# One tap moved from VectorE, two-bank gelus, scales in the weights and a new order of steps in a Mamba and feed-forward layer

## The chip, the cores and the metric

One Trainium2 chip, one core. The time is that of the whole program on the device, in microseconds. The engines are TensorE (PE in the profile, its weight loads PEld), VectorE (DVE), ScalarE (ACT), GpSimd (POOL) and SyncE (SP), which here only issues DMAs.

## The reference

One layer on x of 32 sequences x 256 steps x 128 channels, all in float32:

```
xz = x @ W_in.T ;  u, z = split(xz)                       # 256 inner channels each
u  = silu(causal_conv(u, 4 taps per channel) + conv_b)
B, C, d = split(u @ W_x.T)                                # 16, 16 and 1 columns
dt = softplus(d * W_dt + b_dt)
h[t] = exp(dt[t] * A) * h[t-1] + (u[t] * dt[t]) * B[t]    # 256 channels x 16 states
y  = sum_over_states(h * C) + u * D ;  y = (y * silu(z)) @ W_out.T
x1 = layernorm(x + y)
a  = silu((x1 @ w1) * s1) * ((x1 @ w2) * s2)              # 512 hidden
a  = gelu((a @ h1) * t1) ;  a = gelu((a @ h2) * t2)
out = layernorm(x1 + (a @ w3) * s3)
```

The w, h matrices are ternary numbers times 8; s1, s2, t1, t2 are scales of one number for each hidden column.

## The kernel before, in words

The 8192 rows are cut into NB = 16 blocks of TB = 512 columns (two sequences), with channels on the 128 partitions. The state of one block is 256 x 16 = 4096 rows, that is 32 tiles of 128 partitions, handled in 16 steps `v` of two tiles each.

Every engine runs the same `rounds`: round j runs over the 16 steps, scans block j, and lays the other stages of four other blocks between its steps: the intake of block I = j+2 (first projection and convolution), the front of block A = j+1 (z, the rows of B and C, dt), the back of F = j-1 (out projection, norm, gate and up projections, the first hidden layer h1, the start of h2), and the tail of T = j-2 (rest of h2, w3, last norm, store). The order on each engine is written out by hand as `if v == ...` lines in each engine's `run`. Engines meet only in semaphores.

In one step, VectorE makes two products U = X * xdr (L765; X is the PSUM bank that holds B for the step's states, xdr comes by DMA) and two scans hb = scan(dA, U) (L778). ScalarE makes dA = exp(dtr * negA) (`decay`, L456) some eight tiles ahead (AHEAD), in a ring of DA_RING = 10. GpSimd multiplies both hb by C (`output_term`, L384) into pb, and TensorE sums them over states into bank Y0 or Y1 (`sum_group`, L853). X is refilled three times a round by ScalarE (`fill_X`, L466): fill 0 needs the last U of the round before, and VectorE's first U of the next round needs fill 0.

The convolution of inner channels 0 to 127 is done on VectorE: ScalarE writes the first tap with the bias into `conv` (`conv_first`, L470) and VectorE adds three more, reading the projection in its bank (`taps`, L714). For channels 128 to 255 ScalarE makes the products of all taps (`conv_second`, L480 and L486) into `xtap`, slices 1 to 3 of `hid`, and GpSimd adds them (`add_tap`, L398).

The norm of the first half goes over four engines: `out_proj` (TensorE, L906), `variances` (ScalarE, L559), `rsqrt` (GpSimd, L389 and L391), `scaled` into `x1` (VectorE, L728), `turn_x1` (TensorE, L913), a copy into `x1T` (ScalarE, L656). Then TensorE makes the gate and up projections (L866, L869), ScalarE the silu and a scaled copy (L677, L680), GpSimd their product (L423), TensorE the hidden layers (`hidden`, L862: four outputs m of four matmuls each), and ScalarE a gelu of each bank (L554), whose `scale` is a column of `sc_sb`. `add_x1` (L886) and `down` (L894) end the tail's matmuls. The last norm's residual is read from x1T too, two rounds after it was written for block T, before block F's copy overwrites it.

Silu, gelu and exp lie in different function tables of ScalarE; the profile shows an ACT_TABLE_LOAD at each switch.

The DMAs of a round are all issued by SP in one order: among them store_steps (dts and xds to DRAM), spread_steps (dtr and xdr, 256 KB each, back in replicated form), spread_B and spread_C.

Of the kernel before, what the change touches and what calls it, by code (L numbers as in the profile page):

```python
# [37 lines left out]

CW, CB, DP, WD, BD = 0, 4, 5, 6, 7
# [6 lines left out]

def states_of(k):

    return (0, 0, 1, 1, 1, 1, 0, 0)[k]


def build(nc, xT, win, wx, chp, alog, cwrow, sel, rep, wout, w1, w2, h1, h2, w3, scales, cent_in, ident_in, out):
    with ExitStack() as ctx:
# [19 lines left out]
        sc_sb = sb("sc_sb", [P, 5, NH])  # L73
        negA = sb("negA", [P, TILES])
        sel_sb = sb("sel_sb", [P, PARITIES, 2 * SD])
        rep_sb = sb("rep_sb", [P, PARITIES, P])
        diagD = sb("diagD", [P, NC, P])
# [32 lines left out]

        xtap = hid[:, 1:TAPS, :]
        yo = sb("yo", [P, NT, DM])
# [11 lines left out]
        Y = [ps(f"Y{c}", [P, TB]) for c in range(NC)]  # L124
        G = [ps(f"G{i}", [P, TB]) for i in range(3)]
# [4 lines left out]
        s_zero, s_aexp, s_aneg = sem("s_zero"), sem("s_aexp"), sem("s_aneg")  # L130
        s_sc, s_raw, s_w3x, s_wop, s_wo, s_w3p, s_w3c = (sem("s_sc"), sem("s_raw"), sem("s_w3x"), sem("s_wop"), sem("s_wo"),
# [4 lines left out]
        s_ip, s_conv0, s_tap, s_c1, s_xs = sem("s_ip"), sem("s_conv0"), sem("s_tap"), sem("s_c1"), sem("s_xs")  # L136
        s_conv1, s_xtap, s_tap1 = sem("s_conv1"), sem("s_xtap"), sem("s_tap1")
# [25 lines left out]
        def x_of(b):  # L163

            return x1T[:] if b == 1 else xT_sb[:]
# [8 lines left out]
        G0, G1, G2, Y0, Y1 = G[0][:], G[1][:], G[2][:], Y[0][:], Y[1][:]  # L174
# [9 lines left out]
        BH2 = (G1, G2, G0, G1)  # L184

# [43 lines left out]
        def _(sp):  # L229
# [30 lines left out]
            sp.dma_start(rep_sb[:], rep).then_inc(s_rep, 16)  # L260
# [4 lines left out]
            sp.dma_start(sc_sb[:], scales).then_inc(s_sc, 16)  # L265
            load_xT(1)
            sp.wait_ge(s_rows, 1)
# [28 lines left out]
            sp.dma_start(w1_sb[:], w1).then_inc(s_weights, 16)  # L296
            sp.dma_start(w2_sb[:], w2).then_inc(s_weights, 16)
            sp.dma_start(h1_sb[:], h1.rearrange("(c p) m -> p c m", p=P)).then_inc(s_weights, 16)
# [65 lines left out]
        def _(pool):  # L364
# [80 lines left out]
        def _(act):  # L445
# [145 lines left out]
            for u in range(2):  # L591
                decay(0, u)
# [536 lines left out]
```

## Time and profile before

| | |
|---|---|
| times of three runs | 1041.04, 1045.28, 1045.74 us (median 1045.28) |
| profiled execution | 1041.06 us, of it the span of the instructions 1039.2 us |
| granted TensorE clock | 0.974 of full speed, mean over the span |
| moved by DMA | 184.13 MB, mean 177 GB/s |

Busy time is the time in which an engine has at least one instruction at work; on TensorE the ends of matmuls are modelled. A round can be measured as the distance between two equal instructions of neighbouring rounds. An instruction's duration is some 0.1 us longer than the distance to the next one, since neighbours overlap; costs are therefore best taken from distances.

### The profile page before, as it was taken

The page shows a single profiled execution, that of the slowest core. Times are in us where ns is not written, and L with a number is a line of the kernel's source. Part 1 is how long each engine was busy: PE and PEld are TensorE (multiplying, and loading weights), DVE is VectorE, ACT ScalarE, POOL GpSimd, SP SyncE. Part 2 cuts the span into 40 slices and gives each one's busy share as a digit, 9 for nine tenths or more (in the row PEclk, how much of TensorE's full clock was granted, in tenths as well). Part 3 has the DMA queues.
Part 4 walks back from the last instruction along what each step waited for, and adds up shares of the span by engine and source line. Part 5 has one row for each costly group of instructions (what it writes and reads, how often), then busy time and mean ns, then how long its engine had stood idle before and what let it go on. Part 6 is the DMA issues. An engine that isn't in the chain of part 4 may idle for free.

```text
span 1039.2 us, 13592 instructions
## 1 busy us (share of the span) xinstructions
PE 967.8 (93%) x3852; PEld 428.7 (41%) x3852; DVE 952.1 (92%) x1143; ACT 909.6 (88%) x1544; POOL 841.5 (81%) x497
## 2 busy tenths in 40 slices
PE   5956899999999999999999999999999999998998
PEld 2313335353444435343443535344443534444454
DVE  2899999999999999999999999999999999999500
ACT  5397799999999999999999999999999999997342
POOL 1478898979889897989889897988989798988420
PEclk8688899999999999999999999999999999999999
DMA  4959294784829386593939478392948657392000
GB/s 138 277 175 295 73 294 122 206 233 125 268 88 303 96 244 192 157 267 91 284 84 306 126 200 239 114 274 84 292 114 239 199 155 251 90 301 71 0 11 10
DMA packets 110428, 184.13 MB, mean 177 GB/s; under 512 B 12944, under 2 KB 23696, under 8 KB 110352
## 3 DMA queue, kind: packets, MB, share of 16 engines
q1 hardware_dynamic: 109824, 182.94, 61.1%
q8 instruction: 30, 0.49, 0.2%
q14 instruction: 46, 0.38, 0.1%
q10 hardware_dynamic: 528, 0.32, 0.1%
HBM read 161.19 MB, written 22.02 MB: 176 GB/s over the span
## 4 chain that ended last, share of the span: by engine, by line
PE 26%; issue 24%; DVE 22%; ACT 22%; POOL 5%; DMA 0%; ACTq 0%; DVEq 0%; POOLq 0%; SPq 0%
DVE hb L778 11%; ACT dA L456 9%; DVE U L765 8%; PE G L862 6%; PE G L894 4%; PE Y L853 3%; PE G L866 2%; POOL pb L384 2%; PE Y L862 2%; ACT hid L486 2%; PE G L869 2%; POOL hid L423 1%; ACT xds L519 1%; PE Y L869 1%; ACT dts L519 1%
## 5 line engine op out<-in xcount | busy, mean ns | idle before, releaser
L384 POOL TENSOR_TENSOR pb<-hb,crep 128x1024 f32<-128x1024 f32 x256 | 602.2, 2363 | 110.1 <-DVE hb L778 99.5
L778 DVE TENSOR_TENSOR_SCAN hb<-dA,U 128x512 f32<-128x512 f32 x512 | 595.0, 1205 | 0.0
L456 ACT ACTIVATE dA<-dtr,negA 128x510 f32<-128x510 f32 x500 | 320.9, 711 | 5.9 <-DVE hb L778 5.4
L765 DVE TENSOR_TENSOR U<-X,xdr 128x512 f32<-128x512 f32 x500 | 319.4, 686 | 3.6 <-ACT X L466 2.4
L862 PE MATMUL G<-g,h_sb 128*128 128x512 f32 x512 | 234.2, 601 | 0.0
L862 PE MATMUL G<-hid,h_sb 128*128 128x512 f32 x384 | 173.1, 601 | 0.8 <-ACT g L680 0.8
L853 PE MATMUL Y<-pb,sel_sb 128*32 128x512 f32 x1024 | 138.9, 614 | 19.0 <-POOL pb L384 19.0
L862 PEld LDWEIGHTS G<-g,h_sb 128*128 128x128 f32 x512 | 93.6, 190 | 138.1 <-issue 136.4
L862 PEld LDWEIGHTS G<-hid,h_sb 128*128 128x128 f32 x384 | 70.5, 190 | 103.7 <-issue 101.9
L423 POOL TENSOR_TENSOR hid<-hid,g 128x512 f32<-128x512 f32 x64 | 80.7, 1272 | 13.8 <-ACT g L680 13.7
L853 PEld LDWEIGHTS Y<-pb,sel_sb 128*32 128x32 f32 x1024 | 20.7, 108 | 98.3 <-issue 64.6
L554 ACT ACTIVATE hid<-G,sc_sb 128x512 f32<-128x512 f32 x64 | 40.9, 684 | 20.9 <-PE G L862 20.6
L862 PE MATMUL Y<-hid,h_sb 128*128 128x512 f32 x128 | 57.5, 592 | 0.0
L554 ACT ACT_TABLE_LOAD x44 | 56.5, 1283 | 0.8
L894 PE MATMUL G<-w_sb,hid 128*128 128x128 f32 x480 | 56.1, 275 | 0.0
L456 ACT ACT_TABLE_LOAD x43 | 55.2, 1283 | 0.8
L894 PEld LDWEIGHTS G<-w_sb,hid 128*128 128x128 f32 x480 | 54.8, 192 | 0.2 <-issue 0.2
L866 PE MATMUL G<-x1T,w_sb 128*128 128x512 f32 x96 | 51.5, 619 | 0.0
L398 POOL TENSOR_TENSOR conv<-conv,hid 128x510 f32<-128x510 f32 (+2 forms) x42 | 48.2, 1148 | 2.7 <-ACT hid L486 2.6
L367 POOL TENSOR_TENSOR dts<-dts,xds 128x512 f32<-128x512 f32 x30 | 38.3, 1276 | 5.2 <-ACT xds L526 5.2
L677 ACT ACTIVATE hid<-G,sc_sb 128x512 f32<-128x512 f32 x48 | 32.9, 685 | 9.2 <-PE G L866 8.1
L374 POOL TENSOR_TENSOR xds<-dts,xs 128x512 f32<-128x512 f32 x31 | 39.4, 1272 | 1.3
(141 smaller groups left out, 1116.5 us busy)
## 6 DMA issues: line engine op xcount, KB each, us to landing
dtr<-scr_dt SPq DMA_DIRECT2D x252, 256.0 KB, 7.2
xdr<-scr_xd SPq DMA_DIRECT2D x252, 256.0 KB, 7.1
brep<-scr_rows SPq DMA_DIRECT2D x32, 256.0 KB, 6.1
crep<-scr_rows SPq DMA_DIRECT2D x32, 256.0 KB, 8.1
scr_dt<-dts SPq DMA_DIRECT2D x32, 256.0 KB, 4.3
scr_xd<-xds SPq DMA_DIRECT2D x32, 256.0 KB, 4.2
xres<-xT_d SPq DMA_DIRECT2D x16, 256.0 KB, 5.5
xT_sb<-xT_d SPq DMA_DIRECT2D x15, 256.0 KB, 2.7
```

Of the source, the lines that this page charges most:

```text
L374: nc.gpsimd.tensor_tensor(xds[:, c, :], dts[:, c, :], xs[:, b % 2, c, :], ALU.mult).then_inc(s_xd, 1)
L384: nc.gpsimd.tensor_tensor(pb[:, qs:qs + 2, :], hb[:, hs:hs + 2, :], crep[:, b % 2, g:g + 1, :].to_broadcast([P, 2, TB]), ALU.mult).then_in ...
L398: nc.gpsimd.tensor_tensor(acc, acc, halves(xtap[:, s - 1, :])[:, :, 0:SEQ - s], ALU.add).then_inc(s_tap1, 1)
L423: nc.gpsimd.tensor_tensor(hid[:, m, :], hid[:, m, :], up[:, m, :], ALU.mult).then_inc(s_hid, 1)
L456: nc.scalar.activation(halves(dA[:, decay_slot(b, u), :])[:, :, 1:SEQ], halves(BREP[q] if by_product(b, k) else dtr[:, slot, q, :])[:, :, ...
L554: nc.scalar.activation(o[:, m, :], banks[m], ACT.Gelu, scale=sc_sb[:, kind, m:m + 1]).then_inc(s_done, 1)
L765: nc.vector.tensor_tensor(U[i][:], X[:], xdr[:, slot, q + i, :], ALU.mult).then_inc(s_u, 1)
L778: nc.vector.tensor_tensor_scan(hb[:, 2 * (v % H_PAIRS) + i, :], dA[:, decay_slot(j, u), :], U[i][:], 0.0, ALU.mult, ALU.add).then_inc(s_h, 1)
L853: last = nc.tensor.matmul(Y[c][rows32, :], sel_sb[:, e, :], pb[:, (GT * k + q) % (2 * P_PAIRS), :], start=False, stop=(k % (GROUPS // NC) ...
L862: last = nc.tensor.matmul(to, w[:, k, m * P:(m + 1) * P], x[:, k, :], start=(k == 0), stop=(k == NH - 1))
L866: nc.tensor.matmul(BGATE[m], w1_sb[:, m * P:(m + 1) * P], x1T[:], start=True, stop=True).then_inc(s_ga, 1)
L894: last = nc.tensor.matmul(tile_of(BW3, t), tile_of(g2[:, k, :], t), w3_sb[:, k, :], start=False, stop=(k == NH - 1), skip_group_check=True)
```

## The change

It does these things at once.

- **Scales.** s1, s2, t1, t2 are multiplied into w1, w2, h1, h2 once by GpSimd (`scale_plain`, `scale_hidden`), from rows `srow` broadcast by DMA into g1. Silu, copy and gelu then have no scale operand. w1, w2, h1 and the rows are loaded at the start; h2 later.
- **Gelu.** One instruction for two adjacent banks (G and Y are now one tensor GY), 128x1024, in all rounds that scan. Those of h1 are placed after decay tile 32 instead of at step 11.
- **Tap.** From block 2 on, one of VectorE's three taps is taken away: ScalarE writes its product into slice 0 of hid (`tap_first`), GpSimd adds it to conv (`add_tap0`), before VectorE's other two.
- **x1T** has two buffers.
- **Orders.** `rsqrt` of the first norm at step 3 instead of 4; `scaled` into x1 before the U pair of step 5 instead of behind it; turn_x1 before add_x1; out_proj before z_proj; fill_X(A, 0) after decay tile 34 instead of ahead of tile 36; fill_X(j, 2) between Abs and Relu; conv_first at step 13; hidden output 2 of h1 at step 10, ahead of a sum_group; at the start, negA and the first four decays before the second half's softplus.
- **Small.** The two silus of the convolution are one, 128x1024. rep_sb and diagD share memory with other tensors.

```diff
+POOL_TAPS = 1
+def taps_before(b):
+    return 3 * b if b < 2 else 6 + (3 - POOL_TAPS) * (b - 2)
-        x1T = sb("x1T", [P, TB])
+        x1T = sb("x1T", [P, 2, TB])
+        srow = g1
+        xtap0 = [hid[:, 0, :]]
+        GY = ps("GY", [P, 3 + NC, TB])
+        G, Y = [GY[:, i, :] for i in range(3)], [GY[:, 3 + c, :] for c in range(NC)]
+        BH1_2 = (GY[:, 0:2, :], GY[:, 2:4, :])
+        BH2_2 = (GY[:, 1:3, :], GY[:, 0:2, :])
...
             load_xT(1)
+            sp.dma_start(flat(srow[:, 0:3, :]), scales[:, 0:3 * HID].to_broadcast([P, 3 * HID])).then_inc(s_weights, 16)
+            sp.dma_start(w1_sb[:], w1).then_inc(s_weights, 16)
+            sp.dma_start(w2_sb[:], w2).then_inc(s_weights, 16)
+            sp.dma_start(h1_sb[:], h1.rearrange("(c p) m -> p c m", p=P)).then_inc(s_weights, 16)
...
+            def add_tap0(b, i):
+                pool.wait_ge(s_conv0, b + 1)
+                pool.wait_ge(s_xtap0, POOL_TAPS * (b - 2) + i + 1)
...
+                nc.gpsimd.tensor_tensor(acc, acc, halves(xtap0[i])[:, :, 0:SEQ - s], ALU.add).then_inc(s_tap0, 1)
+            def scale_plain(w, i):
+                pool.wait_ge(s_weights, 16 * 4)
+                nc.gpsimd.tensor_tensor(w[:], w[:], srow[:, i, :], ALU.mult).then_inc(s_wsc, 1)
+            def scale_hidden(w, i, half):
...
+                o = w[:, 2 * half:2 * half + 2, :]
+                nc.gpsimd.tensor_tensor(o, o, srow[:, i:i + 1, :].to_broadcast([P, 2, HID]), ALU.mult).then_inc(s_wsc, 1)
...
-                    if v == 4 and back:
+                    if v == 3 and back:
                         rsqrt(var1, ve1, rs1, s_var1, F + 1, s_rs1, 2 * F + 2)
...
+                    if v == 15 and intake and back:
+                        for i in range(POOL_TAPS):
+                            add_tap0(I, i)
+                    if v == 0 and j == 1:
+                        for i in range(POOL_TAPS):
+                            add_tap0(A, i)
...
+                    if v == 13 and j == 0:
+                        scale_hidden(h2_sb, 3, 0)
+                    if v == 15 and j == 0:
+                        scale_hidden(h2_sb, 3, 1)
                     if scan:
                         output_term(j, v)
...
+            def tap_first(b):
+                if b > 2:
+                    act.wait_ge(s_h1, 4 * (b - 3) + 4)
+                for i in range(POOL_TAPS):
+                    nc.scalar.activation(xtap0[i], bank_in(b), ACT.Copy, scale=chp_sb[:, 0, CW + i:CW + i + 1]).then_inc(s_xtap0, 1)
...
+            def gelu(o, bank2, s_in, s_done, b, m, n):
+                if o is g2 and b + 3 < NB:
+                    act.wait_ge(s_tap1, 3 * (b + 1) + m + n - 1)
+                act.wait_ge(s_in, 4 * b + m + n)
+                nc.scalar.activation(flat(o[:, m:m + n, :]), bank2, ACT.Gelu).then_inc(s_done, n)
...
-                    if v == 14 and front:
-                        fill_X(A, 0)
+                    if v == (13 if back else 14) and intake:
+                        conv_first(I)
+                        tap_first(I)
...
+                        if u == 32 and back and scan:
+                            gelu(g1, flat(BH1_2[0]), s_h1, s_g1, F, 0, 2)
+                            gelu(g1, flat(BH1_2[1]), s_h1, s_g1, F, 2, 2)
+                        if u == 34 and front:
+                            fill_X(A, 0)
...
-                            silu_conv(A, 0)
-                            silu_conv(A, 1)
+                            nc.scalar.activation(flat(xs[:, A % 2, :, :]), flat(conv[:]), ACT.Silu).then_inc(s_xs, 2)
...
-                        softplus_lines(A, 1)
-                        fill_X(j, 2)
+                        softplus_lines(A, 1, lambda: fill_X(j, 2))
...
             def taps(b):
-                for s in range(1, TAPS):
+                moved = POOL_TAPS if b > 1 else 0
+                for s in range(1, TAPS - moved):
...
+                    if moved:
+                        dve.wait_ge(s_tap0, POOL_TAPS * (b - 1))
...
+                        if v == 5 and back:
+                            scaled(x1, BOUT, rs1, s_rs1, 2 * F + 2).then_inc(s_x1, 1)
                         k, q = divmod(2 * v, GT)
...
-                    if v == 0 and front and j > 0:
+                    if v == (0 if tail else 1) and front and j > 0:
                         taps(A)
...
+                    if v == 2 and back:
+                        out_proj(F)
                     if v == (2 if back else 4) and front:
...
+                    if v == 4 and back:
+                        turn_x1(F)
                     if v == 4 and tail:
...
+                    if v == 10 and back:
...
+                        hidden(BH1[2], h1_sb, 2, hid, s_hid, s_h1, F)
```

## Rows read from the trace of the kernel before

**Rows 1.** Stages: length, busy PE, PEld, DVE, ACT, POOL, then clock, DMA.

```profile
486.00:545.50 59.50, 57.78 (x238) 25.63 (x237) 59.33 (x72) 57.25 (x98) 53.09 (x32) 1.00 0.71 192
```

**Rows 2.** Timeline of VectorE: start, us, what, idle time before it.

```profile
89.96 2.28 DVE L714 SCALAR_TENSOR_TENSOR conv<-Y,chp_sb,conv 128x510 f32<-128x510 f32 x3
...
148.66 2.29 DVE L714 SCALAR_TENSOR_TENSOR conv<-Y,chp_sb,conv 128x510 f32<-128x510 f32 x3
...
505.58 2.28 DVE L714 SCALAR_TENSOR_TENSOR conv<-Y,chp_sb,conv 128x510 f32<-128x510 f32 x3
507.78 1.29 DVE L765 TENSOR_TENSOR U<-X,xdr 128x512 f32<-128x512 f32 x2
508.97 2.32 DVE L778 TENSOR_TENSOR_SCAN hb<-dA,U 128x512 f32<-128x512 f32 x2
...
522.06 1.27 DVE L765 TENSOR_TENSOR U<-X,xdr 128x512 f32<-128x512 f32 x2
523.24 0.68 DVE L728 TENSOR_TENSOR x<-Y,rs 128x512 f32<-128x512 f32 x1
...
559.20 2.33 DVE L778 TENSOR_TENSOR_SCAN hb<-dA,U 128x512 f32<-128x512 f32 x2
561.61 1.30 DVE L765 TENSOR_TENSOR U<-X,xdr 128x512 f32<-128x512 f32 x2
```

**Rows 3.** Timeline of TensorE, the same round.

```profile
522.39 0.66 PE L886 MATMUL G<-ident,x1T 128*128 128x128 f32 x4 [0.40 <-ACT hid L554]
523.98 0.66 PE L913 MATMUL Y<-ident,x 128*128 128x128 f32 x4 [0.93 <-DVE x L728]
...
548.38 1.06 PE L853 MATMUL Y<-pb,sel_sb 128*32 128x512 f32 x8 [0.29 <-POOL pb L384]
```

**Rows 4.** Groups of ScalarE's instructions: count, busy us, mean ns.

```profile
L554 ACT ACTIVATE hid<-G,sc_sb 128x512 f32<-128x512 f32 x64 | 40.9, 684 | 20.9 <-PE G L862 20.6
...
L500 ACT ACTIVATE zs<-G 128x512 f32<-128x512 f32 x32 | 18.8, 588 | 0.9 <-PE G L819 0.9
...
L496 ACT ACTIVATE xs<-conv 128x512 f32<-128x512 f32 x31 | 17.9, 622 | 0.2
...
L505 ACT ACTIVATE zs<-zs 128x1024 f32<-128x1024 f32 x16 | 16.7, 1047 | 0.0
```

**Rows 5.** Timeline of ScalarE around the gelus of h1 and fill 0.

```profile
556.54 0.69 ACT L554 ACTIVATE g<-Y,sc_sb 128x512 f32<-128x512 f32 x1 [0.80 <-PE Y L862]
557.25 1.28 ACT L456 ACT_TABLE_LOAD   x1
558.54 2.55 ACT L456 ACTIVATE dA<-dtr,negA 128x510 f32<-128x510 f32 x4
561.00 0.58 ACT L466 ACTIVATE X<-brep 128x512 f32<-128x512 f32 x1
```

**Rows 6.** Timeline of GpSimd, end of round 0 and a middle round, and a group.

```profile
80.62 9.31 POOL L384 TENSOR_TENSOR pb<-hb,crep 128x1024 f32<-128x1024 f32 x4
...
508.90 1.11 POOL L398 TENSOR_TENSOR conv<-conv,hid 128x508 f32<-128x508 f32 x1
...
L398 POOL TENSOR_TENSOR conv<-conv,hid 128x506 f32<-128x506 f32 x14 | 15.2, 1083 | 0.0
```

**Rows 7.** Issues of dtr (500 to 565 us), the first one's and all landing times.

```profile
546.62 2.45 SPq L257 DMA_DIRECT2D dtr<-scr_dt  x4
...
dtr<-scr_dt SPq DMA_DIRECT2D x1, 256.0 KB, 3.1
...
DMA to landing us min/median/max: 3.1/7.8/10.6
```

**Rows 8.** The start, in TensorE's and ScalarE's timelines.

```profile
18.79 1.23 PE L918 MATMUL G<-dts,rep_sb 32*128 32x512 f32 x3 [3.76 <-DVE dts L738]
...
20.99 1.26 ACT L456 ACTIVATE dA<-G,negA 128x510 f32<-128x510 f32 x2
```

**Rows 9.** VectorE's timeline behind its last scan.

```profile
982.75 0.69 DVE L723 TENSOR_TENSOR gT<-Y,zs 128x512 f32<-128x512 f32 x1 [7.01 <-PE Y L853]
```

More of the change, by code:

```diff
@@ L518, in softplus_lines @@
                 for f, o in ((ACT.Abs, soft), (ACT.Relu, dts)):
+                    if between is not None and f == ACT.Relu:
+                        between()
                     nc.scalar.activation(o[:, c, :], BDT, f, bias=chp_sb[:, c, BD:BD + 1],
@@ L589, in _ @@
             act.wait_ge(s_aneg, 1)
+            act.wait_ge(s_dtb, 1)
+            softplus_part(0, ACT.Abs)
+            softplus_part(0, ACT.Relu)
+            softplus_rest(0)
             act.wait_ge(s_zero, 3)
-            for u in range(2):
+            softplus_part(1, ACT.Abs)
+            softplus_part(1, ACT.Relu)
+            for u in range(GT):
                 decay(0, u)
+            softplus_rest(1)
             fill_X(0, 0)
-            for u in range(2, AHEAD):
+            for u in range(GT, AHEAD):
                 decay(0, u)
@@ L616, in run @@
                             decay(A, u - TILES)
+                        if u == 32 and back and scan:
[3 more added lines that the diff above has]
+                            fill_X(A, 0)
+                    if v == 11 and back and not scan:
+                        for m in range(NH):
+                            gelu(g1, BH1[m], s_h1, s_g1, F, m, 1)
                     if v == 3 and scan:
@@ L640, in run @@
                     if v == 1 and tail:
-                        gelu(g2, 3, BH2, s_h2, s_g2, T, (0, 1))
-                    if v == 1 and scan and j > 0:
+                        if scan:
+                            gelu(g2, flat(BH2_2[0]), s_h2, s_g2, T, 0, 2)
+                        else:
+                            for m in (0, 1):
+                                gelu(g2, BH2[m], s_h2, s_g2, T, m, 1)
+                    if v == (1 if tail else 2) and scan and j > 0:
                         start_sum(j, 0)
@@ L646, in run @@
                     if v == 4 and tail:
-                        gelu(g2, 3, BH2, s_h2, s_g2, T, (2, 3))
+                        if scan:
+                            gelu(g2, flat(BH2_2[1]), s_h2, s_g2, T, 2, 2)
+                        else:
+                            for m in (2, 3):
+                                gelu(g2, BH2[m], s_h2, s_g2, T, m, 1)
                     if v == 5 and front and not back:
@@ L691, in run @@
                     if v == 8 and front:
-                        softplus_lines(A, 1)
-                        fill_X(j, 2)
+                        softplus_lines(A, 1, lambda: fill_X(j, 2))
                         softplus_logs(A, 1)
-                    if v == 14 and intake:
-                        conv_first(I)
-                    if v == 11 and back:
-                        gelu(g1, 2, BH1, s_h1, s_g1, F, range(NH))
                     if v == 15 and intake and not back:
@@ L765, in run @@
                                 nc.vector.tensor_tensor(U[i][:], X[:], xdr[:, slot, q + i, :], ALU.mult).then_inc(s_u, 1)
-                        if v == 5 and back:
-                            scaled(x1, BOUT, rs1, s_rs1, 2 * F + 2).then_inc(s_x1, 1)
                         if v == 9 and tail:
@@ L992, in run @@
                             add_x1(T)
-                    if v == 4 and back:
-                        turn_x1(F)
                     if v == 4 and tail and j <= NB:
@@ L1064, in run @@
                         in_proj(I)
-                    if v == 11 and back:
-                        if front:
-                            pe.wait_ge(s_pre, 4 * A)
-                        hidden(BH1[2], h1_sb, 2, hid, s_hid, s_h1, F)
                     if v == 12 and back:
```

108 lines of the change are left out of this document (51 added, 57 removed).

## The prediction

> **What bounds the kernel now.** I read the busy time by stage first [rows 1]. A middle round of 59.5 us has VectorE busy for 59.33 us, TensorE for 57.78, ScalarE for 57.25 and GpSimd for 53.09: VectorE has no room, TensorE and ScalarE have some 2 us each, GpSimd 6.
>
> Next I read VectorE's timeline [rows 2]. From the taps at 148.66 to those at 505.58 lie six rounds, 356.92 us, so a round is 59.49. The first such distance, from 89.96 to 148.66, is 58.70: that round has no last norm. Three taps cost 2.20 us (505.58 to 507.78), 0.735 each. There is one short wait: the pair of scans begun at 559.20 would let the next U begin 2.24 us later (its 2.33 less some 0.09 of overlap), at 561.44, but it begins at 561.61. It waits 0.17 us for fill 0 of X, which ScalarE ended at 561.58 [rows 5]. So two loops are closed at almost the same length: VectorE's own work, 59.49 - 0.17 = 59.32 us, and a loop over TensorE and ScalarE that ends in that fill.
>
> The second loop is seen in TensorE's and ScalarE's timelines [rows 3, 5]. TensorE waits 0.40 us for a gelu of h2 before add_x1, 0.93 for x1 from VectorE, and 0.29 for pb at 548.38; otherwise it works on until the last output of h1, whose gelu begins at 556.54. Then come a table load, four decays and fill 0, and VectorE's U, taps and x1 close the loop. Whoever shortens VectorE's work alone meets this loop at once.
>
> **The change, part by part.**
>
> *Tap.* VectorE loses 0.735 us in rounds 1 to 14, where blocks 2 to 15 are convolved: 14 x 0.735 = 10.3 us. ScalarE gains one copy from a bank with a scale: 684 ns like its gelus [rows 4], less 0.08 of overlap, 0.61. GpSimd gains one add, 1.08 us [rows 6]; its 53.1 becomes 54.2 of 58.6. The add stands at step 15 ahead of an output_term. What hides it is GpSimd's idle time, 6 us a round, and that TensorE's sum of this term is two hidden outputs away; with GpSimd full, all behind it would come 1.08 us later.
>
> *x1 and TensorE's order.* `scaled` moves ahead of a pair of U, so x1 is 523.24 - 522.06 = 1.18 us earlier [rows 2], if rs1 is there; rsqrt at step 3 sees to that. Out_proj ahead of z_proj feeds ScalarE's variances, which ScalarE reaches later anyway: zero. turn_x1 ahead of add_x1 puts add_x1's 0.5 us behind x1. Output 2 of h1 ahead of the sum hides the wait of 0.29 [rows 3]. From fill 0 over x1 to the last output of h1 that is -0.735 - 1.18 + 0.5 - 0.29 = -1.7 us.
>
> *Gelus and fill 0.* A two-bank gelu isn't in the trace. From below it is one bank without scale, 588 ns, and what 512 more columns cost, 1047 - 622 = 425 ns: 1.01 us; from above it is two of today's, 1.37 [rows 4]. I take 1.05, the row of the same width. In place of 0.69 it adds 0.36 us behind the last output of h1. Then table load, one decay, conv_first (0.66, a copy like the tap's), tap_first and one more decay are 1.28 + 0.62 + 0.66 + 0.61 + 0.62 = 3.79 us up to fill 0, against 561.00 - 557.25 = 3.75 now [rows 5]. Fill 0 is 0.4 us later behind the last output of h1, and the loop over fill 0 and x1 is 59.49 - 1.7 + 0.4 = 58.2 us.
>
> A third loop runs over the gelus of h2. ScalarE's way from the last output of h1 to the gelu for which add_x1 waits changes by 0.36, + 0.61 for tap_first, - 0.62 for decay 32, which now lies ahead, + 0.04, - 0.2 for the first pair of h2, + 0.45 since add_x1 waits for a whole pair: + 0.65. TensorE's way behind it loses the turn and the wait for x1: add_x1 to the end of turn_x1 is 523.98 + 0.5 - 522.39 = 2.1 us now and 0.5 then, -1.6, and the 0.29 [rows 3]. That loop is 59.49 + 0.65 - 1.9 = 58.25 us.
>
> *VectorE's own loop* is then 59.32 - 0.735 = 58.58 us, 0.3 above both. The margin is thin, but VectorE stays the bound, and its 0.17 us wait for fill 0 goes too, in 13 rounds (2 to 14): 2.2 us.
>
> The Trainium skill (Perfetto Trace Analysis, Optimizing Scalar/DVE Operations) says the reverse of the merge: where ScalarE isn't saturated but causes bubbles on other engines, breaking instructions up may let work be done sooner. The 0.40 us before add_x1 is such a bubble. By that rule the third loop, which the merge lengthens, would decide; this is the first rival.
>
> *Scales.* Four silus and four copies a round lose 0.1 us each (684 against 588 ns, rows 4), but ScalarE waits there for TensorE's next bank: zero in the rounds. In the last chain some three of them lie on the way: -0.3 us.
>
> *Fill 2* comes one softplus line earlier; VectorE wasn't seen waiting for it: zero.
>
> *Decay 32 ahead of the gelus.* It needs the first dtr of the next block, issued at 546.62 and landed 3.1 us later, at 549.7 [rows 7]. ScalarE gets there at 552.6 (556.54, less its wait of 0.80, three gelus of 0.6 and the table load). Covered by 2.9 us: zero.
>
> *Start.* The first decays began at 20.99, with all of the softplus ahead of them; the replicated dts is there at 18.79 + 1.2 = 20.0 [rows 8]. They start then: -1.0 us. The loads of 2.4 MB that move ahead of the first rows of B and C take 13 us at the page's mean of 177 GB/s, and about half in a burst; I take them as hidden behind the convolution and softplus of block 0, and keep 3 us, once, for the range. Scaling w1, w2, h1 costs GpSimd 2 x 1.27 + 2 x 2.33 = 7.2 us while it has nothing else.
>
> *h2 at the end of round 0.* Here GpSimd isn't idle: four output_terms from 80.62 to 89.93 [rows 6], 2.33 each, the last of them 3.5 us behind its scans. Two scalings (2.33 each) and add_tap0 (1.08) are put ahead of its next work: add_tap0 ends at 89.93 + 4.66 + 1.08 = 95.7, less 1.0 from the start, 94.7. VectorE's taps of block 2, now one step later, would start at 89.96 + 3.42 - 1.0 = 92.4 [rows 2]. They wait 2.3 us: +2.3, once. The bounds are 0, if GpSimd's lag is taken up earlier, and 3.5.
>
> *End.* When the scans end TensorE is further ahead by 1.18 + 0.29 - 0.5 = 0.97 us, and the chain behind the last scan is TensorE's: the gate waits 7.01 us for it [rows 9]. I take -0.9, and the -0.3 above.
>
> Sum: -10.3 - 2.2 - 1.0 + 2.3 - 1.2 = -12.4 us. The profiled execution took 1041.06 us (span 1039.2 and 1.9 around it), which gives 1028.7. The median of the three runs is 1045.28, 4.2 above the profiled one, and would give 1032.9; the three runs lie at both ends of that gap (1041.04, 1045.28, 1045.74). I take the middle, 1043.2, less 12.4: 1031.
>
> **The rivals.**
>
> *ScalarE and TensorE decide the round.* If the two-bank gelu takes 1.37 us, the loop over fill 0 gets 0.3 longer and the loop over the gelus of h2 1.0, as three pairs stand in it: 59.2 against 58.58. For it speaks how thin the margins are; against it that the same width in SBUF took 1047 ns. It costs 13 x 0.6 = 8 us of the gain: 1039.
>
> *GpSimd's add blocks VectorE.* Each add_tap0 would hold VectorE for its 1.08 us, 14 x 1.08 = +15.1, and the sum is +2.7: 1046. Against it: a pair of scans beside such an add (508.97, the add from 508.90) took 2.32 us, like one elsewhere (559.20, 2.33) [rows 2, 6]. The Trainium skill (the same section) warns that the two share an SBUF read port, so that offloading between them might not help; by it this rival would hold.
>
> *Slower: dtr comes too late for decay 32.* The place is ScalarE ahead of the gelus of h1; their delay reaches TensorE's next matmuls and fill 0. 2.9 us are covered by today's landing, 0.8 by ScalarE's present wait for the last output of h1, 0.3 by the margin of the loops. From a landing of 3.1 + 4.0 = 7.1 us on, each further us costs one in each of 13 rounds; at 8.1 us the gain is gone. The landings of dtr in that stretch have median 7.8 and maximum 10.6 us [rows 7]. With 10.6 it is 13 x 3.5 = 45 us worse: 1076. Against it: the first piece starts the burst and meets an empty queue, since it follows GpSimd's dt.
>
> *No effect.* VectorE's taps would wait for add_tap0 in every round, if GpSimd, which goes into step 15 some 1 us behind the scans, came 2 us later than now. Then start and end alone remain: 1043.2 - 1 = 1042. Against it: its 3 us of idle time around steps 0 to 3.
>
> **Numbers.** My case 0.68 (1025 to 1036 by itself), the loops 0.17 (to 1041), blocked VectorE 0.04, dtr late 0.04, no effect 0.07. The range 1023 to 1041 leaves out the last three and a little below. A measurement here can't tell less than 0.5%, 5.2 us, from no change, so faster begins below 1040. Faster 0.84, within 0.5% 0.10, slower 0.06.
>
> **What would show it.** Right: taps of two at a distance of 58.6 us in rounds 2 to 14, no wait of the first U for fill 0, one wait of some 2.3 us for add_tap0 at the first taps of two, scans that start 1 us earlier, gelus of 1.05 us. Wrong: VectorE waiting for X every round (first rival), scans over 2.4 us a pair beside L398's like (second), the exp of tile 32 waiting for a DMA (third), taps waiting for GpSimd every round (fourth). Most likely to spoil the number: a gelu over two banks above 1.1 us, or which level, 1041 or 1045, the median falls on.

## The result, and the profile after

The changed kernel takes 1033.67 us (median of five runs, 1032.09 to 1035.66) against 1045.28 (five runs, 1041.04 to 1045.74): ratio 0.9903, 95% interval 0.9879 to 0.9928. This ratio, like those below, is built from all the runs; it is that of the two means, 1033.91 and 1043.98, and not that of the two medians (0.9889). Predicted: 1031.0, range 1023 to 1041. The profiled execution took 1034.61 us, span 1032.7. One later execution of the kernel before, beside places_back and h2_in_round1, took 2471.68 us and is left out of their ratios.

**The round.** One stage of the profile of after, with the columns of [rows 1]:

```profile
481.50:540.00 58.50, 57.08 (x237) 25.43 (x236) 58.37 (x71) 55.99 (x94) 53.95 (x33) 1.00 0.75 195
```

Now VectorE's timeline of after, to be read against [rows 2]:

```profile
97.85 1.63 DVE L786 SCALAR_TENSOR_TENSOR conv<-GY,chp_sb,conv 128x510 f32<-128x510 f32 x2 [2.86 <-POOL conv L419]
...
152.47 1.60 DVE L786 SCALAR_TENSOR_TENSOR conv<-GY,chp_sb,conv 128x510 f32<-128x510 f32 x2
...
557.01 2.31 DVE L850 TENSOR_TENSOR_SCAN hb<-dA,U 128x512 f32<-128x512 f32 x2
559.25 1.26 DVE L839 TENSOR_TENSOR U<-X,xdr 128x512 f32<-128x512 f32 x2
...
855.66 1.60 DVE L786 SCALAR_TENSOR_TENSOR conv<-GY,chp_sb,conv 128x510 f32<-128x510 f32 x2
...
966.38 2.32 DVE L850 TENSOR_TENSOR_SCAN hb<-dA,U 128x512 f32<-128x512 f32 x2
976.95 0.69 DVE L795 TENSOR_TENSOR gT<-GY,zs 128x512 f32<-128x512 f32 x1 [8.24 <-PE GY L925]
```

From 152.47 to 855.66 lie twelve rounds, 58.60 us each (59.49 before). VectorE is busy for all but 0.1 us of one. The U at 559.25 follows its scans after 2.24 us, so the wait for fill 0 is gone. The taps take 1.51 us up to the next U where three took 2.20 [rows 2]: the moved tap gives back 0.69 us, not 0.735. Before the taps of round 1 there is one wait of 2.86 us for GpSimd's add.

TensorE, ScalarE and GpSimd of after, a middle round, against [rows 3, 5, 6]:

```profile
579.18 0.66 PE L985 MATMUL GY<-ident,x 128*128 128x128 f32 x4 [1.42 <-DVE x L800]
579.67 0.60 PE L958 MATMUL GY<-ident,x1T 128*128 128x128 f32 x4
```

```profile
551.67 1.02 ACT L615 ACTIVATE g<-GY 128x1024 f32<-128x1024 f32 x1
553.24 1.02 ACT L615 ACTIVATE g<-GY 128x1024 f32<-128x1024 f32 x1 [0.54 <-PE GY L934]
...
558.05 0.59 ACT L518 ACTIVATE X<-brep 128x512 f32<-128x512 f32 x1
```

```profile
559.60 1.12 POOL L419 TENSOR_TENSOR conv<-conv,hid 128x506 f32<-128x506 f32 x1
```

A gelu over two banks takes 1.02 us. Fill 0 ends at 558.64, 0.6 before its U starts. TensorE now waits for VectorE's x1 by 1.42 us and no longer for a gelu before add_x1: the slack has moved to the engines that don't set the round.

**Where the time went,** between the two profiled executions: start +2.8 us; the rest of round 0 and round 1 +1.0; twelve rounds -10.67; rounds 14 and 15 up to the end of the last scan -0.2; behind it +0.5. The sum is -6.5, which is their difference. The profiled execution of before lies at the low end of its runs and that of after near the high end of its own, so the gain between the means is larger, 10.1 us.

**The start,** VectorE and GpSimd of after:

```profile
19.35 2.19 DVE L810 TENSOR_TENSOR dts<-dts,xds 128x512 f32<-128x512 f32 x1 [8.90 <-ACT xds L598]
21.58 2.72 DVE L813 TENSOR_TENSOR xds<-dts,xs 128x512 f32<-128x512 f32 x1
26.75 1.30 DVE L835 TENSOR_TENSOR U<-GY,brep 128x512 f32<-128x512 f32 x2 [2.45 <-PE GY L990]
...
46.30 2.45 DVE L786 SCALAR_TENSOR_TENSOR conv<-GY,chp_sb,conv 128x510 f32<-128x510 f32 x3 [2.00 <-ACT conv L522]
```

```profile
16.21 2.49 POOL L423 TENSOR_TENSOR w_sb<-w_sb,g 128x512 f32<-128x512 f32 x2 [9.18 <-DMA h_sb<-h_d]
18.65 5.10 POOL L429 TENSOR_TENSOR h_sb<-h_sb,g 128x1024 f32<-128x1024 f32 x2
```

The taps of block 1 come at 46.30; before they came at 43.53. Two VectorE instructions, both of whose inputs are in SBUF, took 2.19 and 2.72 us, where they took 0.69 each before, beside GpSimd's scalings of h1, which took 2.55 each where 2.33 had been reckoned.

**The end,** TensorE of after in round 15, and the windows there (columns as in [rows 1]; the clock is the last number but two):

```profile
929.25 1.11 PE L985 MATMUL GY<-ident,x 128*128 128x128 f32 x4 [3.22 <-DVE x L800]
...
931.01 5.72 PE L966 MATMUL GY<-w_sb,hid 128*128 128x128 f32 x32
```

```profile
918.00:925.00 7.00, 7.00 (x40) 4.16 (x39) 7.00 (x9) 6.33 (x16) 4.84 (x3) 1.00 1.08 287
...
930.00:935.00 5.00, 5.00 (x25) 5.00 (x24) 5.00 (x7) 4.28 (x6) 3.39 (x2) 0.50 1.06 247
```

```profile
944.67 0.69 DVE L800 TENSOR_TENSOR yo<-GY,rs 128x512 f32<-128x512 f32 x1 [0.61 <-POOL rs L410]
```

TensorE waited 3.22 us for x1, the granted clock fell from 1.00 to 0.50 (1.2 GHz) towards the end of that wait, the down projection took 5.72 us, and VectorE (last row) then waited 0.61 us for the last norm that depends on it.

### The profile page after: what moved, and what is told of

Read it like the earlier page. It is cut to its first block, busy times and chain, and to the rows that moved or that the text cites. A ratio compares the mean times of both kernels' runs of the same rounds, so it can differ in the third digit from the quotient of the medians.

```text
span 1032.7 us, 13619 instructions
## 1 busy us (share of the span) xinstructions
PE 961.2 (93%) x3852; PEld 428.7 (42%) x3852; DVE 943.9 (91%) x1129; ACT 891.4 (86%) x1486; POOL 867.8 (84%) x517
## 4 chain that ended last, share of the span: by engine, by line
PE 51%; issue 17%; ACT 14%; DVE 11%; POOL 3%; DMA 1%; SPq 1%; ACTq 0%; DVEq 0%; POOLq 0%
PE GY L934 23%; ACT dA L508 6%; PE GY L925 6%; DVE hb L850 5%; PE GY L966 5%; PE GY L938 5%; PE GY L941 4%; DVE U L839 4%; PE GY L906 2%; ACT hid L545 2%; POOL pb L403 2%; ACT L508 1%; DVE gT L795 1%; PE GY L881 1%; PE GY L985 1%
## 5 line engine op out<-in xcount | busy, mean ns | idle before, releaser
L934 PE MATMUL GY<-g,h_sb 128*128 128x512 f32 x512 | 234.2, 601 | 0.0
L934 PE MATMUL GY<-hid,h_sb 128*128 128x512 f32 x512 | 228.7, 600 | 0.9 <-ACT g L756 0.7
L925 PE MATMUL GY<-pb,sel_sb 128*32 128x512 f32 x1024 | 138.5, 613 | 14.7 <-POOL pb L403 14.6
L934 PEld LDWEIGHTS GY<-g,h_sb 128*128 128x128 f32 x512 | 93.5, 190 | 138.2 <-issue 138.2
L934 PEld LDWEIGHTS GY<-hid,h_sb 128*128 128x128 f32 x512 | 93.6, 190 | 136.4 <-issue 122.5
L938 PE MATMUL GY<-x1T,w_sb 128*128 128x512 f32 x128 | 69.4, 624 | 0.0
L941 PE MATMUL GY<-x1T,w_sb 128*128 128x512 f32 x128 | 66.1, 599 | 0.9 <-ACT hid L754 0.9
L966 PE MATMUL GY<-w_sb,hid 128*128 128x128 f32 x480 | 58.1, 281 | 0.0
L966 PEld LDWEIGHTS GY<-w_sb,hid 128*128 128x128 f32 x480 | 56.9, 198 | 0.0
L754 ACT ACTIVATE hid<-GY 128x512 f32<-128x512 f32 x64 | 37.9, 592 | 17.2 <-PE GY L938 17.2
L615 ACT ACTIVATE hid<-GY 128x1024 f32<-128x1024 f32 (+1 forms) x36 | 33.5, 930 | 21.0 <-PE GY L934 20.7
## 6 DMA issues: line engine op xcount, KB each, us to landing
xres<-xT_d SPq DMA_DIRECT2D x16, 256.0 KB, 10.1
```

What stands on the lines that cost most here:

```text
L615: nc.scalar.activation(flat(o[:, m:m + n, :]), bank2, ACT.Gelu).then_inc(s_done, n)
L925: last = nc.tensor.matmul(GY[rows32, 3 + c, :], sel_sb[:, e, :], pb[:, (GT * k + q) % (2 * P_PAIRS), :], start=False, stop=(k % (GROUPS // ...
L934: last = nc.tensor.matmul(to, w[:, k, m * P:(m + 1) * P], x[:, k, :], start=(k == 0), stop=(k == NH - 1))
L938: nc.tensor.matmul(BGATE[m], w1_sb[:, m * P:(m + 1) * P], x1T[:, b % 2, :], start=True, stop=True).then_inc(s_ga, 1)
L941: nc.tensor.matmul(BUP[m], w2_sb[:, m * P:(m + 1) * P], x1T[:, b % 2, :], start=True, stop=True).then_inc(s_up, 1)
L966: last = nc.tensor.matmul(tile_of(BW3, t), tile_of(g2[:, k, :], t), w3_sb[:, k, :], start=False, stop=(k == NH - 1), skip_group_check=True)
```

## The experiments

Eleven kernels were run, each timed in several rounds beside the kernel before on the same chip (`after_again` is the changed kernel once more; median of before 1042.64 us for the first four, 1041.79 for the next four, then 1041.92 for two and 1041.48 for the last). The round is read as the distance of equal taps.

| kernel | median us | ratio, 95% interval | round us |
|---|---|---|---|
| tap_alone | 1039.37 | 0.9955 (0.9937 to 0.9972) | 59.18 |
| tap_back | 1042.18 | 0.9995 (0.9978 to 1.0011) | 59.42 |
| norm_order_back | 1037.35 | 0.9941 (0.9920 to 0.9963) | 58.79 |
| gelu_one_bank | 1033.77 | 0.9903 (0.9871 to 0.9935) | 58.60 |
| after_again | 1033.21 | 0.9910 (0.9894 to 0.9926) | 58.60 |
| scale_at_step4 | 1030.32 | 0.9886 (0.9869 to 0.9902) | 58.60 |
| scale_gaps_negA | 1029.98 | 0.9884 (0.9869 to 0.9899) | 58.60 |
| filler | 1030.54 | 0.9888 (0.9873 to 0.9903) | 58.60 |
| places_back | 1037.48 | 0.9950 (0.9935 to 0.9966) | 58.99 |
| h2_in_round1 | 1031.31 | 0.9891 (0.9876 to 0.9907) | 58.60 |
| wout_first | 1028.19 | 0.9864 (0.9840 to 0.9887) | 58.60 |

**1. tap_alone:** the kernel before with nothing but the tap moved.

```diff
+                    if v == 15 and intake and back:
+                        add_tap0(I, 0)
+                    if v == 0 and j == 1:
+                        add_tap0(A, 0)
...
                     if v == 14 and intake:
                         conv_first(I)
+                        tap_first(I)
...
-                for s in range(1, TAPS):
+                moved = POOL_TAPS if b > 1 else 0
+                for s in range(1, TAPS - moved):
...
-                    if s == 1:
-                        dve.wait_ge(s_conv0, b + 1)
-                    else:
-                        dve.wait_ge(s_tap, 3 * b + s - 1)
+                    dve.wait_ge(s_conv0, b + 1)
+                    if moved:
+                        dve.wait_ge(s_tap0, POOL_TAPS * (b - 1))
+                    if s > 1:
+                        dve.wait_ge(s_tap, taps_before(b) + s - 1)
```

> The kernel before with the tap moved and nothing else. Theory of the loops: a round of VectorE's own work would be 58.6 us, but the loop over ScalarE and TensorE through the gelus of h2 gets tap_first's 0.6 us on ScalarE and loses only TensorE's wait for x1, so a round becomes about 59.0 us (from 59.49) and VectorE waits some 0.4 us a round for fill 0. Total some 6 us below before. Rival (only VectorE's work counts): a round of 58.6 us, as in the full change, 11 to 12 us below before.

Measured: a round of 59.18 us, 1039.37. A tap was taken from VectorE and the round lost only 0.31 us. VectorE's timeline of tap_alone shows what holds it; the wait for GpSimd stands in each of the rounds 3 to 14:

```profile
326.43 1.63 DVE L744 SCALAR_TENSOR_TENSOR conv<-Y,chp_sb,conv 128x510 f32<-128x510 f32 x2 [0.26 <-POOL conv L406]
...
556.97 2.33 DVE L808 TENSOR_TENSOR_SCAN hb<-dA,U 128x512 f32<-128x512 f32 x2
559.39 1.30 DVE L795 TENSOR_TENSOR U<-X,xdr 128x512 f32<-128x512 f32 x2
```

The loop over the other engines did take over, and it holds VectorE in two places. Behind the scans of 556.97 the next U begins after 2.42 us, where 2.24 is enough in rounds without a wait: the short wait for fill 0 is still there, as in before. The new wait, for the add of the moved tap, is 0.34 us by the same reading. The two taps take 1.55 us for 2.20, so the round is 0.65 shorter by the tap and 0.34 longer by the new wait: the 0.31 measured. The theory had the round (59.0) nearly right, but saw only the wait at fill 0. GpSimd's timeline of tap_alone says where the new wait comes from: there the add waits for ScalarE's copy,

```profile
443.65 1.08 POOL L406 TENSOR_TENSOR conv<-conv,hid 128x506 f32<-128x506 f32 x1 [1.90 <-ACT hid L496]
```

whereas after's L419 begins right behind GpSimd's own work.

**2. tap_back:** the change without the tap.

```diff
-POOL_TAPS = 1
+POOL_TAPS = 0
```

> The changed kernel with the tap back on VectorE (three taps, no tap_first, no add_tap0). Theory: VectorE's own loop of 59.3 us sets the round, without its wait for fill 0; the 2.9 us wait for add_tap0 in round 1 is gone. So 14 x 0.735 less 2.9 = 7.4 us above the changed kernel, some 3 us below before. Rival (the orders give the time and the tap little): a round of 58.6 to 58.8 us, within 2 us of the changed kernel.

Measured: 59.42 us a round, 1042.18, no difference from before. VectorE of tap_back:

```profile
506.42 2.44 DVE L786 SCALAR_TENSOR_TENSOR conv<-GY,chp_sb,conv 128x510 f32<-128x510 f32 x3
508.77 1.29 DVE L839 TENSOR_TENSOR U<-X,xdr 128x512 f32<-128x512 f32 x2
```

The orders remove the wait for fill 0 (0.20 us a round with the slightly later U behind it). But three taps now take 2.35 us up to the next U, 0.15 more than in before. The edit left on the taps is that all but the first wait for two semaphores where one was; that this costs the 0.15 is likely, but wasn't tried apart. So this kernel isn't quite the orders alone. Neither half of the change is worth much by itself (0.31 and 0.07 us a round); together they are worth 0.89: 0.69 for the tap and 0.20 for fill 0.

**3. norm_order_back:** rsqrt at step 4, `scaled` behind the U pair, turn_x1 behind add_x1.

```diff
-                    if v == 3 and back:
+                    if v == 4 and back:
                         rsqrt(var1, ve1, rs1, s_var1, F + 1, s_rs1, 2 * F + 2)
...
-                        if v == 5 and back:
-                            scaled(x1, BOUT, rs1, s_rs1, 2 * F + 2).then_inc(s_x1, 1)
...
+                        if v == 5 and back:
+                            scaled(x1, BOUT, rs1, s_rs1, 2 * F + 2).then_inc(s_x1, 1)
...
-                    if v == 4 and back:
-                        turn_x1(F)
                     if v == 4 and tail:
...
+                    if v == 4 and back:
+                        turn_x1(F)
```

> The changed kernel with the first norm's order as before: rsqrt at step 4, scaled behind the U pair of step 5, turn_x1 behind add_x1. Theory: x1 comes 1.2 us later and add_x1's 0.5 us goes ahead of it, so the loop over x1, TensorE and fill 0 gets 0.7 us longer than its 58.2: 58.9 us a round, with VectorE waiting 0.3 us for fill 0 each round: 4 us above the changed kernel. Rival (TensorE has 1.4 us to spare at x1 and takes it up): the round stays at 58.6 us, within 1 us.

Measured: 58.79 us, 1037.35. TensorE of norm_order_back again waits ahead of add_x1, now longer than in [rows 3]:

```profile
522.91 0.66 PE L958 MATMUL GY<-ident,x1T 128*128 128x128 f32 x4 [1.62 <-ACT hid L615]
```

The order of the norm is worth 0.19 us a round. It reaches VectorE through fill 0, as the theory says. Its timeline, and ScalarE's:

```profile
558.60 2.33 DVE L850 TENSOR_TENSOR_SCAN hb<-dA,U 128x512 f32<-128x512 f32 x2
561.00 1.30 DVE L837 TENSOR_TENSOR U<-X,xdr 128x512 f32<-128x512 f32 x2
```

```profile
560.38 0.59 ACT L518 ACTIVATE X<-brep 128x512 f32<-128x512 f32 x1
```

The U begins 2.40 us after its scans instead of 2.24, right behind the fill, which ends at 560.97, and it takes 0.03 longer up to the next scans. The theory holds in kind; its 0.3 us was 0.19.

**4. gelu_one_bank:** 128x512 gelus in the same places, those of h2 too.

```diff
-                            gelu(g1, flat(BH1_2[0]), s_h1, s_g1, F, 0, 2)
-                            gelu(g1, flat(BH1_2[1]), s_h1, s_g1, F, 2, 2)
+                            for m in range(NH):
+                                gelu(g1, BH1[m], s_h1, s_g1, F, m, 1)
...
                     if v == 1 and tail:
-                        if scan:
-                            gelu(g2, flat(BH2_2[0]), s_h2, s_g2, T, 0, 2)
-                        else:
-                            for m in (0, 1):
-                                gelu(g2, BH2[m], s_h2, s_g2, T, m, 1)
+                        for m in (0, 1):
+                            gelu(g2, BH2[m], s_h2, s_g2, T, m, 1)
```

> The changed kernel with a gelu of 128x512 for each bank, at the same places. My theory: VectorE sets the round, so it stays at 58.60 us, and only the waits of TensorE and ScalarE change: within 1 us of the changed kernel. By the rule of the Trainium skill (Perfetto Trace Analysis, Optimizing Scalar/DVE Operations) broken-up gelus let TensorE go on sooner: TensorE's waits get shorter, and the time too if TensorE is the bound, by up to 0.4 us a round, 5 us below the changed kernel. If the merge is what gives ScalarE its room: above it, 59 us a round.

Measured: 58.60 us and 1033.77. The merge neither costs nor gives anything here, and TensorE's wait for x1 in a middle round is 1.42 us with and without it: broken-up gelus didn't let TensorE go on sooner.

**5. places_back:** on ScalarE, the gelus of h1, fill 0, conv_first and tap_first at the steps that they had before.

```diff
-                    if v == (13 if back else 14) and intake:
-                        conv_first(I)
-                        tap_first(I)
+                    if v == 14 and front:
+                        fill_X(A, 0)
...
-                        if u == 32 and back and scan:
-                            gelu(g1, flat(BH1_2[0]), s_h1, s_g1, F, 0, 2)
-                            gelu(g1, flat(BH1_2[1]), s_h1, s_g1, F, 2, 2)
-                        if u == 34 and front:
-                            fill_X(A, 0)
...
+                    if v == 14 and intake:
+                        conv_first(I)
+                        tap_first(I)
+                    if v == 11 and back and scan:
+                        gelu(g1, flat(BH1_2[0]), s_h1, s_g1, F, 0, 2)
+                        gelu(g1, flat(BH1_2[1]), s_h1, s_g1, F, 2, 2)
```

> The change, with ScalarE's order at the end of a round as before: gelus of h1 at step 11, fill 0 ahead of decay tile 36, the first tap's copy and the new tap's copy at step 14 behind it. My theory, by the loops: the copy for the new tap ends some 2 us later in each round, so GpSimd's add comes later and VectorE waits for it at each taps by 0.3 us: rounds of 58.9 us, and a time of 1037. Rival: these places are worth nothing once the norm's order is changed: rounds of 58.60 us, a time within 1 us of the change's 1033.5. A second rival: the copy becomes so late that the whole tap is lost again: rounds of 59.2 us or more, 1040.

Measured: 1037.48, a round of 58.99, and VectorE of places_back has tap_alone's wait again:

```profile
448.12 1.63 DVE L786 SCALAR_TENSOR_TENSOR conv<-GY,chp_sb,conv 128x510 f32<-128x510 f32 x2 [0.26 <-POOL conv L419]
```

My theory holds. These places, which the prediction booked mainly as a delay of fill 0, are what lets the tap pay: 0.39 us a round. With the norm's 0.19 that is 0.58, just what lies between tap_alone and the change. The places were moved back together; what each of them is worth isn't shown.

**6. after_again and scale_at_step4:** the change once more, and the change with the scalings of w1, w2 and h1 at step 4 of round 0 instead of the start.

```diff
-            scale_plain(w1_sb, 0)
-            scale_plain(w2_sb, 1)
-            scale_hidden(h1_sb, 2, 0)
-            scale_hidden(h1_sb, 2, 1)
             pool.wait_ge(s_soft0, 4)
...
+                    if v == 4 and j == 0:
+                        scale_plain(w1_sb, 0)
+                        scale_plain(w2_sb, 1)
+                        scale_hidden(h1_sb, 2, 0)
+                        scale_hidden(h1_sb, 2, 1)
```

> The changed kernel itself, timed beside the next three on one chip: 1033 to 1034 us, 1% below before.

> The changed kernel with GpSimd's scaling of w1, w2 and h1 moved from the start to step 4 of round 0, where GpSimd waits 9.9 us for a sum. Theory: at the start these four instructions hold VectorE's two instructions with two SBUF operands (dts + soft, dts * xs: 2.19 and 2.72 us in place of 0.69 each). Without them both take 0.69 us, the first U starts 3.5 us earlier, and so does all behind it: 3.5 us below the changed kernel. Rival (the two are long for another reason, or the start is late by the DMAs): they stay at over 2 us, and the time stays within 1 us.

VectorE of after_again, then of scale_at_step4:

```profile
19.74 2.13 DVE L810 TENSOR_TENSOR dts<-dts,xds 128x512 f32<-128x512 f32 x1 [9.18 <-ACT xds L598]
21.90 0.69 DVE L813 TENSOR_TENSOR xds<-dts,xs 128x512 f32<-128x512 f32 x1
```

```profile
19.78 0.69 DVE L811 TENSOR_TENSOR dts<-dts,xds 128x512 f32<-128x512 f32 x1 [9.31 <-ACT xds L599]
20.50 0.69 DVE L814 TENSOR_TENSOR xds<-dts,xs 128x512 f32<-128x512 f32 x1
...
95.83 1.63 DVE L787 SCALAR_TENSOR_TENSOR conv<-GY,chp_sb,conv 128x510 f32<-128x510 f32 x2 [2.87 <-POOL conv L419]
```

With GpSimd idle the pair takes 0.69 each, the taps of block 1 come at 44.63, 2.0 us earlier than in after_again (46.62) and 1.7 earlier than in after, and the time is 2.9 us shorter. The wait for add_tap0 stays.

**7. scale_gaps_negA:** also the h2 scalings at step 9 of round 0, and negA behind the softplus.

> As scale_at_step4, and h2's two scalings moved from steps 13 and 15 of round 0 to step 9, where GpSimd waits 4.7 us for softplus, and negA computed while ScalarE waits for the first replicated dts. Theory: the 2.9 us wait of VectorE for add_tap0 in round 1 goes too, and 0.5 us of ScalarE at the start: 6.9 us below the changed kernel. Rival (GpSimd's lag comes back elsewhere, in the front of block 1): 3.5 to 4.5 us below.

Measured: 1029.98; 3.2 us below after_again where 6.9 were expected. The wait for add_tap0 is gone, but VectorE then waits for TensorE (0.25 us) and for the first norm's rs (0.99); the taps of round 2 come only 1.7 us earlier than in scale_at_step4, and the medians of the two are only 0.3 us apart. The rival was nearer.

**8. filler:** the same, with six matmuls on a free bank (their result isn't used) in front of the turn_x1 of round 15.

> As scale_gaps_negA, with six matmuls on a free bank ahead of turn_x1 in round 15, where TensorE waited 3.2 us for x1; their results are overwritten. Theory: TensorE's granted clock fell to half for 6.8 us right behind that wait, which made down 2 us longer, the last norm 0.6 us late and the last gate 1.2 us late. Without a long wait the clock stays at 1.0 and the time is 1 to 2 us below scale_gaps_negA. Rival (the fall has nothing to do with the wait): the fall is still in the trace, and the time is the same or 0.5 us longer.

Measured: neither the wait nor the fall of the clock is there, and the time is 1030.54: nothing gained. TensorE of filler:

```profile
923.64 5.31 PE L1062 MATMUL GY<-x1T,win_sb 128*128 128x512 f32 x12
928.79 0.60 PE L985 MATMUL GY<-ident,x 128*128 128x128 f32 x4
```

The six matmuls (twelve records) take 5.31 us where the wait was 3.22, so turn_x1 comes some 1.8 us later than it could, and the gate behind the last scan waits 7.86 us, as long as with the fall of the clock (7.79 in scale_gaps_negA) and longer than without (6.57 to 6.59 in four traces). So the filling was too long, and whether one of the right length pays stays open. In nine other traces TensorE waits 2.76 us or more for x1 in round 15; the clock fell with it in five (after, tap_back, gelu_one_bank, scale_gaps_negA, places_back) and not in four.

**9. h2_in_round1:** scale_at_step4, with the h2 scalings at steps 3 and 4 of round 1, and negA behind the softplus.

```diff
-                    if v == 13 and j == 0:
-                        scale_hidden(h2_sb, 3, 0)
-                    if v == 15 and j == 0:
-                        scale_hidden(h2_sb, 3, 1)
+                    if v in (3, 4) and j == 1:
+                        scale_hidden(h2_sb, 3, v - 3)
...
+                            if m == 3 and j == 1:
+                                act.wait_ge(s_wsc, 6)
```

> The change, with the scalings of w1, w2 and h1 at step 4 of round 0, those of h2 at steps 3 and 4 of round 1, and negA behind the softplus. My theory: at the taps of round 1 VectorE waits neither for the new tap nor, later in round 1, for the first norm, since GpSimd's 4.7 us of scalings then lie in front of idle time of 1.5 us and of pairs that TensorE uses two steps later. The taps of round 2 come at 147.5 us instead of 150.44, and the time is 1027.5. Rival: the start of round 1 is set by TensorE's order at the end of round 0 anyway, and the lag of GpSimd only moves: taps of round 2 at 149 us or later, 1030.

Measured: 1031.31; the rival holds. VectorE of h2_in_round1 doesn't wait for the add any more, but for TensorE, and TensorE in turn had waited for ScalarE:

```profile
95.25 0.69 DVE L796 TENSOR_TENSOR gT<-GY,zs 128x512 f32<-128x512 f32 x1 [1.30 <-PE GY L926]
```

```profile
85.11 2.04 PE L1078 MATMUL GY<-cent,yo 128*128 128x128 f32 x8 [4.07 <-ACT wout_sb L695]
```

In the trace of after this wait is 4.07 us as well; in that of before, TensorE's timeline has 0.43:

```profile
81.17 2.04 PE L1007 MATMUL G<-cent,yo 128*128 128x128 f32 x8 [0.43 <-ACT wout_sb L628]
```

wout_sb holds the out projection's weights, made once in round 0: ScalarE copies them out of a bank, and TensorE needs this bank for the weights w3. The change put fill 0 of the next round in front of this copy (step 13 of round 0), and fill 0 there waits 3.54 us for VectorE's last U.

**10. wout_first:** h2_in_round1, with that copy ahead of the decays of step 13.

```diff
+                    if v == 13 and j == 0:
+                        act.wait_ge(s_wop, 1)
+                        nc.scalar.activation(flat(wout_sb[:]), G0[:, 0:DI], ACT.Copy).then_inc(s_wo, 1)
                     if v == (13 if back else 14) and intake:
                         conv_first(I)
...
-                    if v == 13 and j == 0:
-                        act.wait_ge(s_wop, 1)
-                        nc.scalar.activation(flat(wout_sb[:]), G0[:, 0:DI], ACT.Copy).then_inc(s_wo, 1)
```

> As h2_in_round1, with ScalarE's copy of wout_sb in round 0 ahead of the decays of step 13 and so ahead of fill 0, which waits there for VectorE's last U. My theory: the 4.07 us that TensorE waited for this copy made the intake of block 2, the sums and the copy of w3 late, and so replaced the wait for GpSimd's add at the start of round 1: now the gate of round 1 waits for nothing instead of 1.30 us, the first norm's x not 0.18, and the taps of round 2 come at 149.2 us or earlier instead of 150.70. Time 1029.5 beside 1031.3, or 1.5 us below. Rival: something else is late by as much (rs of the first norm, or fill 0 at 147.25, which waited 0.57 us): the taps of round 2 stay at 150.4 or later and the time at 1031.

Measured: 1028.19 us, ratio 0.9864. TensorE of wout_first has no wait there, and VectorE none from 47 us to the taps of round 2 but 0.7 for a fill, which come 4.2 us earlier than in h2_in_round1:

```profile
80.58 1.80 PE L1078 MATMUL GY<-cent,yo 128*128 128x128 f32 x8
```

```profile
146.54 1.60 DVE L787 SCALAR_TENSOR_TENSOR conv<-GY,chp_sb,conv 128x510 f32<-128x510 f32 x2
```

My theory holds, and by more than expected. This is the fastest version, 5 us below the change.

## Why the prediction was right, and where it was not

**Right: the round.** Predicted 58.58 us, measured 58.60: one tap less, and no wait for fill 0. The parts are off a little against each other: the tap gave 0.69 us and not 0.735, the wait for fill 0 0.20 and not 0.17. That VectorE's loop and the others were nearly equal before, so that the tap by itself would meet the second loop at once, is shown by tap_alone and tap_back: 0.31 and 0.07 us a round apart, 0.89 together. The gelu of two banks was put at 1.05 us and took 1.02; in gelu_one_bank the round is the same, so the merge doesn't set it, and the first rival, which needed 1.37, didn't come. The second rival fails too: pairs of scans take 2.31 to 2.32 us beside GpSimd's adds. The third: in a middle round ScalarE's decay 32 waits for no dtr. The fourth: no wait for the add in rounds 2 to 14.

**Right in kind, short in size: the wait for add_tap0.** +2.3 predicted, +2.86 measured. The start was taken to shorten this lag by 1.0 and did not.

**Wrong: the start, -1.0 predicted, +2.8 measured.** The step that failed is "Scaling w1, w2, h1 costs GpSimd 7.2 us while it has nothing else". It costs VectorE: GpSimd's scalings held two VectorE instructions up, by 1.5 and 2.0 us; scale_at_step4 gives back 1.7 at the taps of block 1. Counted from the start of dts on VectorE (17.95 in before, 19.35 in after), the taps of block 1 come 25.58 us later in before, 26.95 in after, and 24.57 to 24.85 in four of the five kernels without scalings at the start (25.52 in filler, unexplained). So the earlier decays did give 0.7 to 1.0 us, as the sum has it, and the scalings took 2.1 to 2.4. The other 1.4 us is that dts begins later. Of this 0.8 us isn't the change's at all: tap_alone has the start of before unedited and its taps of block 1 come at 44.32, for its first convolution took 5.26 us where before's took 4.45 in its profiled execution. TensorE of tap_alone:

```profile
6.93 5.26 PE L839 MATMUL G<-xT_sb,yo 128*128 128x512 f32 x8 [0.38 <-POOL yo L419]
```

In the thirteen traces this convolution takes 4.45 to 6.60 us, and that of before is the shortest; so the +2.8 hangs on the trace by more than a microsecond. The rest is small, and was not tried apart: ScalarE's two negA instructions stand 0.5 us ahead of the softplus. In the trace of before TensorE replicated dts from 18.79 us on [rows 8]; in the traces of the change's variants VectorE begins dts only at 18.75 to 20.98, so the first decays could not start where I put them.

**Missed: the copy of wout_sb.** Moving fill 0 to step 13 was weighed only for the rounds. In round 0 it stands ahead of a copy that TensorE waits for: 0.43 us became 4.07. In the change itself it seems hidden behind the wait for add_tap0; h2_in_round1, without that wait, lays it bare, and wout_first has neither. The 3.1 us between these two are the largest gain of a single step among the variants.

**Wrong: the end, -1.2 predicted, +0.5 measured.** The step was "TensorE is further ahead by 0.97 us" when the scans end. The gate waits 8.24 us in the profiled execution, and 6.58 in after_again, where TensorE's clock didn't fall in round 15: so the gain was 0.4 us, not 0.9, and the fall of the clock took 1.7, besides the 0.6 in front of the last norm. The -0.3 for the last gelus and copies was -0.7 (gate to the end of the span: 55.75 us, before 56.45).

The errors are 3.8 us at the start, 0.6 for the wait, 1.7 at the end and 0.9 in the rounds (11.6 with the tap of round 1, for 12.5), of which the wait for the last norm is 0.6; all go the same way. Against them stand 1.3 us less of waiting for fills of X in round 0 (2.36 before, 1.05 after), which the sum did not have. Together that is 5.7 of the 5.9 us between -12.4 and -6.5.

So the sum was right in its largest part, the round, and about twice too large between the two profiled executions. Between the means the gain is 10.1 us, and 9.2 between after_again and the runs of before beside it (1032.94 and 1042.16). That the median came out only 2.7 us above the forecast is in part luck with the level from which the 12.4 was taken.

## What to carry to other kernels

Where two loops have nearly the same length, cost an edit by the longer loop that remains: here a tap taken from VectorE (0.65 to 0.69 us) was worth 0.31 alone, a reordering of the other engines 0.07 alone, and both together 0.89. A wait too short to be listed shows in the distance between two starts. A moved step has to be followed through the first and the last round as well: what waits there, and what is queued behind it, isn't what a middle round shows. And "while the engine has nothing else to do" is not free if a neighbour with two inputs in SBUF works at the same time.

## What the runs showed of the hardware

A VectorE instruction with both inputs in SBUF hardly advances while GpSimd works through a long tensor_tensor: 0.69 us became 2.19 and 2.72, and they end some 0.3 and 0.55 us behind GpSimd's two halves (23.75 the second, about 21.2 the first if they are equal). After_again has the same at the second half:

```profile
16.67 4.64 POOL L429 TENSOR_TENSOR h_sb<-h_sb,g 128x1024 f32<-128x1024 f32 x2
```

GpSimd ends at 21.31, VectorE's first instruction at 21.87, 0.56 us later, and the second takes 0.69 again. In the six traces with the scalings at the start at least one of the two takes 1.25 to 2.77 us, in the seven without them both take 0.69. Scans, products and taps, which have one input in PSUM, show nothing of the kind beside the same engine. The Trainium skill (SBUF — State Buffer, Who interferes with whom) states just this: two SBUF inputs contend with a GpSimd instruction that reads SBUF, an instruction with one doesn't. Every trace here agrees (scans beside the add take 2.31 to 2.32 us a pair), and the section decides against the prediction's second rival.

TensorE's clock can fall with one wait: in a wait of 3.22 us in round 15 of after the granted clock went from 1.00 to 0.50, and 32 matmuls took 5.72 us in place of 3.74. The same wait in after_again, scale_at_step4, h2_in_round1 and wout_first brought no fall. With the wait filled by 5.31 us of matmuls (filler) there was none either, but no time was gained, since the filling was longer than the wait.
